# Splitting the PSUM ring banks of an attention stage: four for row maxima and two for transposed scores, in place of three and three

## The reference

```python
xn = layernorm(x)                                  # no affine part
q = (xn @ wq).reshape(B, T, 32, 16)                # 32 heads of 16
k, v = xn @ wk, xn @ wv                            # one key and one value head (512 x 16) for all
scores = einsum('bqhd,bkd->bhqk', q, k) / sqrt(16) # causal mask, softmax over k
s = einsum('bhqk,bkd->bqhd', softmax(scores), v).reshape(B, T, 512) @ wo
h = linear8bit(xn, W1, b1)                         # 512 -> 2048; rows of x and W quantized to int8
g = silu(linear8bit(h, W2, b2))                    # columns with max over 3 stay in floating point
out = x + s * g
```

## Time and profile before

| | |
|---|---|
| median of 3 runs (lowest, highest) | 870.93 us (869.99, 877.79) |
| profiled execution, its own time | 875.71 us |
| its span | 874.0 us |
| granted TensorE clock, mean | 0.966 |
| TensorE (PE) busy | 799.8 us, 92% |
| TensorE weight loads (PEld) busy | 579.6 us, 66% |
| VectorE (DVE) busy | 675.3 us, 77% |
| ScalarE (ACT) busy | 406.5 us, 47% |
| GpSimd (POOL) busy | 253.5 us, 29% |

### The profile page before, as it was taken

How to read it: one execution, slowest core, us unless ns; L and a number is a source line. 1 busy time by engine, 2 the same in 40 slices (tenths; PEclk the granted TensorE clock), 3 DMA queues, 4 the chain that set the end, 5 groups by cost and what they waited for, 6 DMA issues and landing times. The chain is left out here.

```text
span 874.0 us, 12108 instructions
## 1 busy us (share of the span) xinstructions
PE 799.8 (92%) x4253; PEld 579.6 (66%) x4253; DVE 675.3 (77%) x1116; ACT 406.5 (47%) x682; POOL 253.5 (29%) x331
## 2 busy tenths in 40 slices
PE   3899999999999999999889999999996999999983
PEld 2677655556655665566457878787875888887772
DVE  6898879897798789878535675765656998599967
ACT  2224056665666566666833455445444332143221
POOL 7101125454455445444441001010100000135306
PEclk9999679999999999999999999999997999999997
DMA  5721202322232222231534443412004234024852
GB/s 143 238 99 49 65 23 64 87 77 74 81 88 78 87 79 70 63 99 62 169 126 142 143 152 114 145 53 81 25 24 169 61 120 157 25 85 144 258 200 96
DMA packets 53884, 89.90 MB, mean 103 GB/s; under 512 B 10288, under 2 KB 18496, under 8 KB 52416
## 3 DMA queue, kind: packets, MB, share of 16 engines
q1 hardware_dynamic: 53824, 89.13, 32.6%
HBM read 47.69 MB, written 28.31 MB: 87 GB/s over the span
## 5 line engine op out<-in xcount | busy, mean ns | idle before, releaser
L838 DVE TENSOR_REDUCE rowmax<-ps 128x2 f32<-128x512 f32 (+3 forms) x384 | 215.5, 592 | 48.1 <-PE ps L897 46.4
L759 ACT ACTIVATE probs<-ps 128x512 f32<-128x512 f32 (+1 forms) x352 | 182.1, 559 | 115.2 <-PE ps L910 114.2
L897 PE MATMUL ps<-km,stack 128*128 128x256 f32 (+3 forms) x512 | 154.6, 357 | 2.4 <-PEq L171 1.9
L897 PEld LDWEIGHTS ps<-km,stack 128*128 128x128 f32 (+1 forms) x512 | 97.4, 200 | 71.0 <-DVE rowmax L838 44.4
L910 PE MATMUL ps<-stack,ks 128*128 128x512 f32 (+1 forms) x352 | 134.3, 389 | 9.6 <-DMA stack<-ml 9.6
L741 POOL TENSOR_SCALAR_AFFINE_SELECT probs<-probs 128x512 f32<-128x512 f32 x128 | 79.8, 635 | 115.5 <-ACT probs L759 115.5
L1631 PE MATMUL ps<-big_h 128*128 128x512 f32 x256 | 101.9, 398 | 9.1 <-DVE big_l L1556 9.1
L1303 PE MATMUL ps<-big_h,w1h 128*128 128x512 f32 x256 | 105.2, 411 | 1.4 <-DVE w1l L1174 1.4
L1305 PE MATMUL ps<-big_h,w1l 128*128 128x512 f32 x256 | 101.7, 397 | 0.0
L1304 PE MATMUL ps<-big_l,w1h 128*128 128x512 f32 x256 | 101.1, 395 | 0.0
L1633 PE MATMUL ps<-big_h,big_l 128*128 128x512 f32 x256 | 100.9, 394 | 0.0
(11 more groups left out here) (193 smaller groups left out, 1286.1 us busy)
## 6 DMA issues: line engine op xcount, KB each, us to landing
stack<-big_h SPq DMA_DIRECT2D x128, 64.0 KB, 2.0
projected_rows<-w2t_scratch SPq DMA_DIRECT2D x32, 256.0 KB, 2.6
h_scratch<-hs SPq DMA_DIRECT2D x7, 1024.0 KB, 4.5
hload<-h_scratch SPq DMA_DIRECT2D x14, 512.0 KB, 5.0
xn_scratch<-xa SPq DMA_DIRECT2D x4, 1024.0 KB, 5.2
stack<-big_l SPq DMA_DIRECT2D x64, 64.0 KB, 2.0
xi<-xn_scratch SPq DMA_DIRECT2D x16, 256.0 KB, 2.7
xe_scratch<-xm SPq DMA_DIRECT2D x16, 256.0 KB, 2.3
```

The costliest lines, as they stand in the source:

```text
L759: nc.scalar.activation(probs[:, o:o + nh * w], ps[:, STB[n % NST], 0:nh * w], ACT.Exp).then_inc(s_exp, 1)
L838: nc.vector.tensor_reduce(dst, src, AX_X, ALU.max).then_inc(s_red, 1)
L897: last = nc.tensor.matmul(dst, stack[u % 3][rows, hp, P * qt:P * (qt + 1)], km[rows, u // KT, p0:p0 + npar, keys], start=True, stop=True)
```

## The change

It rewrites one line: the row-maximum pieces rotate through banks 0 to 3, the transposed scores through banks 4 and 5. `NMAX` and `NST` follow from the lengths, and with them every wait and every bank index that uses them. No instruction is added or removed.

```diff
-        MAXB, STB, PVB, MISCB = (0, 1, 2), (3, 4, 5), 6, 7
+        MAXB, STB, PVB, MISCB = (0, 1, 2, 3), (4, 5), 6, 7
         NMAX, NST = len(MAXB), len(STB)
```

## The result

The change made the kernel slower: 882.62 us median against 870.93 us, ratio 1.0123 with a 95% interval of 1.0097 to 1.0149. A second set of runs of the same kernel gave 1.0115 (1.0090 to 1.0141). The forecast was 884 us.

A forecast was written before the change was run, and what follows sets the result against it. VectorE's length nearly set unit 8, TensorE's list units 9 and 10. Late score loads at 0.85 us in 15 units gave 13 us, the fourth bank and tail zero: 884 us on the 870.93 us median, range 873 to 897.

The forecast's parts named there:

- The handover: Score and row-maximum banks: a waiting weight load starts 0.05 us after its bank's reader ends, for ScalarE as for VectorE.
- the three places: Unit 8: loads of scores 6, 10 and 14 wait for exponentials 4, 8 and 12; shift 0.33, 0.55, then 0.6 us.
- The fourth bank at nothing: Row-maximum ring: the fourth bank removes some piece-load waits but is costed at nothing, hidden by the score ring.
- the forecast's other two arguments: Fourth bank: scores 10 and 11, next in TensorE's list, wait longer; in units 9 and 10 TensorE itself makes pieces late.
- The size of a late load: Unit 8, score 6: load 0.33 us later, and everything behind it in TensorE's order moves by 0.33 us.
- The running shift: Unit 8: delay of TensorE's list builds from 0.33 to 0.55 at score 10, 0.6 at score 14, 0.8 at score 19.
- The give-back: End of unit: score 19 adds about 0.2 us; VectorE's slack does not absorb the shift, which reaches the next unit's score 0.
- The sum: Attention: 0.85 us a unit as mean of four kinds, over 15 units, 13 us; unit 8 at 0.8, unit 10 at 1.0.
- Absorbed: Attention: score waits fall into time TensorE would wait for VectorE anyway; 3 us, 874 us in all; chance 0.22.
- The fourth bank wins: Attention: the fourth bank saves 0.53 us a unit where VectorE runs dry, 8.5 us, giving 862 us; chance 0.06.
- Delays add up: Attention: the shortfalls add, as every late load also uncovers the load itself; 27 us, 898 us; chance 0.04.
- The clock: Attention: new pauses bring one more 21 us stretch to TensorE's lower clock level, about 15 us more, 899 us; chance 0.02.

The follow-up runs named there:

- three and two: Changed kernel with three row-maximum banks in place of four, still two score banks, one bank unused: 882.75 us, ratio 1.0119 against the kernel before.

## Why the prediction was right, and where its sizes were off

**The handover and the three places: right.** ScalarE's bank is reloaded 0.05 us after its exponential, and scores 6, 10 and 14 of unit 8 wait, as said. The new wait in the list is 18.2 us in 45 loads and 2.8 us in 16 matmuls; 10 to 25 us in some 60 places were forecast. Here the row is what it says: each of the 45 loads starts within 0.1 us of the end of its exponential. By place, over all units, 3.8 us stand at score 6, 7.2 at score 10 and 5.0 at score 14. Score 19 is loaded 0.05 us behind its exponential in 15 units, mostly with an idle time of 0.14 us that the list leaves out as too short. No load of either ring started less than 0.05 us after the end of its reader, in any of the twelve traces.

**The fourth bank at nothing: right, but partly for a wrong reason.** The unchanged time of three and two shows the zero. My text treated the 44.4 us of the earlier trace rows as TensorE waiting for banks, and forecast that they would fall under 15; they stayed at 45.1. The timeline of after shows why. The first piece load behind a value group, and the reduction four pieces before it, whose bank it takes:

```profile
263.81 0.19 PEld L897 LDWEIGHTS ps<-km,stack 96*128 96x128 f32 x1 [0.84 <-DVE rowmax L838]
```

```profile
261.30 0.43 DVE L838 TENSOR_REDUCE rowmax<-ps 128x2 f32<-128x256 f32 x1 [0.30 <-PE ps L897]
```

The reduction ended at 261.73, the load started at 263.81, 2.1 us later. It did not wait for that bank; the eight value products were streaming, during which the load engine shows idle time, and the name beside it is a release that came long before. Over the whole trace of the kernel before, 10 of the 84 loads of that row, 3.3 of its 44.4 us, start within 0.1 us of the end of the reduction that frees their bank; after, 13 of 88, 3.4 of 45.1 us. The bank itself did act: with or without idle time ahead of them, 50 piece loads of the kernel before start that close behind their reduction, 17 of the changed kernel, 30 with three and two. It was not worth anything, for which the forecast's other two arguments are the likely reason (argued, not tested by a run of its own): at the steps where a piece does wait, a score stands behind it, and in the units with projection TensorE is late by itself.

**The size of a late load: too large.** I added the lateness of weight loads as if it were TensorE's time. Here are the matmuls around score 6, first before, then after:

```profile
256.94 0.40 PE L897 MATMUL ps<-km,stack 96*128 96x512 f32 x1
257.18 0.34 PE L910 MATMUL ps<-stack,ks 128*128 128x384 f32 x1
257.36 0.40 PE L897 MATMUL ps<-km,stack 128*128 128x256 f32 x2
...
257.86 0.64 PE L922 MATMUL ps<-probs,vones 128*32 128x512 f32 x4
```

```profile
261.70 0.40 PE L897 MATMUL ps<-km,stack 96*128 96x512 f32 x1
262.03 0.44 PE L910 MATMUL ps<-stack,ks 128*128 128x384 f32 x1
262.31 0.40 PE L897 MATMUL ps<-km,stack 128*128 128x256 f32 x2
...
262.81 0.64 PE L922 MATMUL ps<-probs,vones 128*32 128x512 f32 x4
```

From the piece to the value group it was 0.92 us and is 1.11: 0.19, where the load lacked 0.33. In the kernel before, the load at 256.94 ran 0.24 us ahead of its matmul at 257.18; the late one starts with it. So 0.24 us of the lateness were lead that nobody needed, and the matmul came 0.09 us late; the next piece follows it after 0.28 us where it was 0.18, another 0.10: the matmul with the late load is itself listed with 0.44 us in place of 0.34. That is the term that was too large in unit 8. The running shift shows at the loads behind the value groups of scores 11 and 14, first before, then after:

```profile
261.73 0.19 PEld L897 LDWEIGHTS ps<-km,stack 96*128 96x128 f32 x1 [0.62 <-DVE rowmax L838]
...
264.07 0.19 PEld L897 LDWEIGHTS ps<-km,stack 96*128 96x128 f32 x1 [0.41 <-DVE rowmax L838]
```

```profile
266.87 0.19 PEld L897 LDWEIGHTS ps<-km,stack 96*128 96x128 f32 x1 [0.63 <-DVE rowmax L838]
...
269.30 0.19 PEld L897 LDWEIGHTS ps<-km,stack 96*128 96x128 f32 x1 [0.41 <-DVE rowmax L838]
```

From the start of the unit (245.62 and 250.41 us) they come at 16.11 and 18.45 us before and at 16.46 and 18.89 after: late by 0.35 and 0.44 us, where the forecast had built up 0.55 and 0.6.

**The give-back: partly there.** For score 19 I counted 0.2 us into the length of every unit. Its load is late, but in units 8 and 9 TensorE waits behind it for the maxima by DMA anyway (the load of score 0 in unit 8: 1.29 us before, 1.20 after), and they depend on VectorE's last reduction, not on score 19. In units 10 and 11 score 0 has no such wait, and the 0.2 us are kept. VectorE's last reduction is the place that the prediction named: at 264.56 it had waited 0.53 us, and after it waits 0.61:

```profile
269.78 0.56 DVE L838 TENSOR_REDUCE rowmax<-ps 128x1 f32<-128x384 f32 x1 [0.61 <-PE ps L897]
```

From the start of the unit it comes at 19.37 us where it came at 18.94: 0.43 later, which is the unit's whole growth. So the shift passes through VectorE's chain and is kept, as said, but only what has built up by then.

**The sum.** Forecast 0.85 us a unit as the mean of the four kinds; measured 2.61 / 4 = 0.65. Unit 8 was forecast at 0.8 (measured 0.43) and unit 10 at 1.0 (0.93). Unit 9, which the prediction put with unit 10 under TensorE, kept only 0.39: score 19 is given back there too, and with the projection between its last scores the load of score 14 comes 1.06 us after the exponential that frees its bank. Unit 11, which it did not work out, kept 0.86. 15 x 0.65 = 9.8 us, against 9.9 us in attention. In medians it was 11.7 us on the first chip and 10.0 on the second, against the 13 forecast. The mechanism accounts for about 10; that the first median came nearer to 13 is luck.

**The rivals.** Absorbed: unit 8 grew by half of its forecast and unit 9 by less than half of the mean, not by nothing. The fourth bank wins: refuted by three and two. Delays add up: no, since a late load costs less than its lateness. The clock: the granted clock stayed at 1.00 in the four units, as in the earlier trace rows, and the new pauses of up to 0.7 us brought no lower level there. In the order with the value products moved, part of attention did run at a lower mean clock (0.86 in a unit), so this rival cannot be waved away for other orders. The Trainium skill (Perfetto Trace Analysis, Optimization Strategy) says that repeated gaps can mean too few buffers. That pointed to the ring whose gaps are in the list, and here it pointed wrong: the gaps were as large with a fourth bank (45.1 against 44.4 us). It holds for the third bank: without it the gaps are 77.7 us, and its absence costs 26 us.

## What to carry to other kernels

Before a bank is taken from a ring, compare each load with the end of the reader one turn nearer: the waits of the trace cannot show a shortage that is not there yet. Before one is given, look up how long before the waiting load its own bank had come free; a total of waits by name may only count the first load behind a long group. And count a late weight load by what comes late behind its matmul (0.19 us here), not by the lateness of the load (0.33).

## What the runs showed of the hardware that was not expected

With the order of TensorE's list exchanged inside a step and no bank changed, the named releaser of about 40 us of idle weight-load time changed from VectorE to ScalarE (44.4 to 3.8, and 0 to 37.4 us). And the steady state is exact: three profiled executions with two score banks, two of them with four row-maximum banks and one with three, took 85.38 us each for the same four units. The clock is less so: in one profiled execution units of the same kind took 22.56 us at a mean granted clock of 1.00 and 24.95 at 0.86.
